# A GNN and mixture-of-experts layer on one core: VectorE's steps rearranged and shortened, and 40 result scatters kept in DRAM and replayed on the POOL queue at the end of the gather stage

## What is computed

```python
edge_index = jnp.stack([src, dst])            # 100000 edges over 6250 nodes, sorted by dst
x = x + _L0_gnn_ref(_layernorm(x, axis=-1), edge_index, L0_gnn_weight, L0_gnn_bias)
x = x + _L0_ffn_ref(_layernorm(x, axis=-1)[None], L0_ffn_gate_w, ..., L0_ffn_b2)[0]

# _L0_gnn_ref(x, ...), D = 256
    summed = jax.ops.segment_sum(x[src], dst, num_segments=n)
    deg = jax.ops.segment_sum(jnp.ones_like(src, dtype=x.dtype), dst, num_segments=n)
    agg = summed / jnp.maximum(deg, 1.0)[:, None]
    out = jnp.concatenate([x, agg], axis=-1) @ weight
    out = out / jnp.linalg.norm(out, axis=-1, keepdims=True)
    return out + bias
# _L0_ffn_ref(h, ...): 8 experts, F = 1024, a capacity for each expert
    probs = jax.nn.softmax(x @ gate_w + gate_b, axis=-1); idx = jnp.argmax(probs, axis=-1)
    pos = (jnp.cumsum(one_hot, axis=0) * one_hot).sum(-1).astype(jnp.int32) - 1
    buf = zeros.at[idx, pos_safe].set(x, mode='drop')
    hmid = jax.nn.relu(jnp.einsum('ecd,edf->ecf', buf, w1) + b1[:, None, :])
    ybuf = jnp.einsum('ecf,efd->ecd', hmid, w2) + b2[:, None, :]
    y_tok = ybuf[idx, pos_g] * (prb * kept)[:, None]
```

## Time and profile before

| | |
|---|---|
| time, median of 3 runs | 1400.24 us (1398.0 to 1404.33) |
| profiled execution | 1398.44 us, span 1396.6 us |
| TensorE busy | 1120.8 us (80%) |
| POOL busy | 907.4 us (65%) |
| VectorE busy | 868.0 us (62%) |
| ScalarE busy | 464.5 us (33%) |

### The profile page before, as it was taken

How to read it: one execution, slowest core, us unless ns; L and a number is a source line. 1 busy time by engine, 2 the same in 40 slices (tenths; PEclk the granted TensorE clock), 3 DMA queues, 4 the chain that set the end, 5 groups by cost and what they waited for, 6 DMA issues and landing times.

```text
span 1396.6 us, 29269 instructions
## 1 busy us (share of the span) xinstructions
PE 1120.8 (80%) x4989; PEld 820.2 (59%) x4990; DVE 868.0 (62%) x3856; ACT 464.5 (33%) x1360; POOL 907.4 (65%) x931
## 2 busy tenths in 40 slices
PE   1076766788889898989888898989898888887786
PEld 1054554566666666666666666666666666654454
DVE  8645454666666666666666666666666666665443
ACT  3511212233333333333333333333333333334342
POOL 3167676677777777777777777777777777731101
PEclk9999798999999999999999999999999999999999
DMA  7686878443444434343433434343434344321111
GB/s 246 199 269 206 249 226 243 148 127 116 131 123 123 130 118 133 115 132 114 128 115 112 121 110 121 110 126 110 125 110 121 114 113 120 113 75 43 47 38 35
DMA packets 113601, 183.38 MB, mean 131 GB/s; under 512 B 21419, under 2 KB 84448, under 8 KB 113584
## 3 DMA queue, kind: packets, MB, share of 16 engines
q0 software_dynamic: 43328, 109.52, 27.2%
q1 hardware_dynamic: 70256, 73.69, 17.6%
HBM read 155.29 MB, written 35.83 MB: 137 GB/s over the span
## 4 chain that ended last, share of the span: by engine, by line
DVE 29%; PE 27%; DVEq 20%; issue 18%; DMA 3%; ACT 2%; ACTq 0%; SPq 0%; POOLq 0%; POOL 0%
PE ps_q L726 14%; PE ps_h L792 7%; DVE sel L1037 6%; DVEq L1301 6%; PE ps_t L800 2%; PE ps_b L811 2%; DVE acc L1046 2%; DVEq L1108 2%; DVEq L894 2%; DMA b_b<-in_L_ffn_b 2%; DVEq L1037 1%; DVEq L1064 1%; DVE row L1150 1%; DVE idx L1033 1%; DVE bn L1156 1%
## 5 line engine op out<-in xcount | busy, mean ns | idle before, releaser
L461 POOL DMA_INDIRECT ring<-xn_d,idx x784 | 788.0, 1005 | 316.5 <-issue 171.5
L726 PE MATMUL ps_q<-ring,sel 128*128 128x257 f32 x1952 | 582.8, 405 | 151.2 <-DVE sel L1037 119.9
L726 PEld LDWEIGHTS ps_q<-ring,sel 128*128 128x128 f32 x1952 | 346.5, 195 | 291.5 <-issue 234.3
L1037 DVE SCALAR_TENSOR_TENSOR sel<-lane,block,dst_t 128x512 f32<-128x512 bf16 x245 | 184.3, 752 | 132.8 <-issue 76.6
L811 PE MATMUL ps_b<-w_sb,hid_t 128*128 x832 | 213.8, 385 | 16.1 <-ACT hid_t L626 16.1
L1046 DVE TENSOR_TENSOR acc<-acc,ps_q 128x257 f32 x245 | 103.2, 421 | 178.4 <-issue 166.9
L792 PE MATMUL ps_h<-w_sb,hid_t 128*128 x416 | 200.0, 608 | 6.2 <-ACT hid_t L594 6.2
L811 PEld LDWEIGHTS ps_b<-w_sb,hid_t 128*128 128x128 f32 x832 | 153.5, 190 | 49.0 <-issue 30.1
L621 ACT ACTIVATE hid<-ps_h 128x512 f32<-128x512 f32 x104 | 62.1, 597 | 190.4 <-PE ps_h L792 190.4
L626 ACT ACTIVATE hid_t<-ps_t,b_t 128x128 f32<-128x128 f32 x416 | 113.2, 383 | 31.5 <-PE ps_t L800 31.5
L792 PEld LDWEIGHTS ps_h<-w_sb,hid_t 128*128 128x128 f32 x416 | 75.5, 191 | 67.4 <-issue 65.2
(11 more groups left out here) (194 smaller groups left out, 1230.0 us busy)
## 6 DMA issues: line engine op xcount, KB each, us to landing
w_sb<-in_L_ffn_w SPq DMA_DIRECT2D x32, 512.0 KB, 9.7
ring<-xn_d,idx POOLq DMA_INDIRECT x784, 2.8
disp_d<-hid SPq DMA_DIRECT2D x8, 1040.0 KB, 7.9
xs<-disp_d SPq DMA_DIRECT2D x53, 130.0 KB
ys<-disp_d SPq DMA_DIRECT2D x53, 130.0 KB
b_b<-in_L_ffn_b SPq DMA_DIRECT2D x53, 128.0 KB
xb<-in_x SPq DMA_DIRECT2D x51, 128.0 KB
out<-row SPq DMA_DIRECT2D x51, 128.0 KB
```

Of the source, the lines that this page charges most:

```text
L461: pool.indirect_dma_start(ring[:, (k % 2) * TQ + j, 0:D], None, xn_d[:, :], bass.IndirectOffsetOnAxis(ap=idx[:, k * TQ + j:k * TQ + j + 1] ...
L726: mm = pe.matmul(ps[:, 0:AW], sel[:, s, j, :], ring[:, (k % 2) * TQ + j, 0:AW], start=(j == 0), stop=(j == TQ - 1), skip_group_check=True)
L1037: dve.scalar_tensor_tensor(out=sel[:, s, :, :], in0=lane[:, :].rearrange("p (j m) -> p j m", j=1).to_broadcast((P, TQ, P)), scalar=block0[ ...
```

## The change

1. **VectorE's register loads.** `dve.load(next_regs, ...)` of eight values at each trip's start goes; each `select_quad` loads the two values of the next quad right after its last selection. TensorE loads two values in each quad instead of eight in one.
2. **Index copies** (L1033, four per trip) go to ScalarE, as two copies per trip.
3. **route** has five steps in place of nine; the copy of the rows to be sent goes to ScalarE (in `exponent`). The square-root refinement of `new_row` goes: ScalarE does four small steps instead. The scaling of the bias by the gate goes to ScalarE (`out_bias`), and `result` has seven steps in place of eight.
4. **choose and finish_row move** from the earlier chains into one chain with `new_row`, behind `select_quad(t, 3)`.
5. **`down` waits** for `count_read` (VectorE has read the counts) in place of `row_ready`. TensorE's `plan` stays as it was, but for the register loads.
6. **Results of the 41 chunks of the gather stage** no longer go through POOL: SP stores each into a DRAM list (`res_d`). At the end of the gather stage POOL loads them back, seven buffers in the ring's place, and scatters 40 of them: 10 ahead of the first late dispatch, 12, 12 and 6 behind the last three dispatches and their results.
7. ScalarE's `prepare_node` moves from a trip's start to the end of the trip before.

```diff
-            def load_ys(t):
+            def keep_result(t):
+                sp.wait_ge(res_ready, chunks(t))
+                sp.dma_start(res_d[ds((t - C0) * P, P), :], ys[:, :]).then_inc(res_kept, 16)
+
+            def load_ys(t, kept=False):
...
-                if not isinstance(t, int):
-                    sp.wait_ge(res_out, 16 * chunks(t))
+                if kept:
+                    sp.wait_ge(res_kept, 16 * chunks(t))
+                elif not isinstance(t, int):
+                    sp.wait_ge(res_out, 16 * (chunks(t) - KEPT))
...
+            def load_replay(r):
+                s, use = r % NRB, r // NRB
+                if use:
+                    pool.wait_ge(replay_out[s], 16 * use)
+                pool.dma_start(rbuf[:, s, :], res_d[(r + 1) * P:(r + 2) * P, :]).then_inc(replay_in[s], 16)
+
+            def replay(r):
+                s, use = r % NRB, r // NRB
+                pool.wait_ge(replay_in[s], 16 * (use + 1))
+                pool.sem_inc(pool_turn, 1)
+                pool.indirect_dma_start(
+                    out[:, :], bass.IndirectOffsetOnAxis(ap=rbuf[:, s, C_NODE:C_NODE + 1].bitcast(I32), axis=0),
+                    rbuf[:, s, 0:D], None, bounds_check=N - 1, oob_is_err=False).then_inc(replay_out[s], 16)
+
+            def replays(part):
+                for r in range(REPLAYS[part - 1] if part else 0, REPLAYS[part]):
+                    replay(r)
+                    if 2 <= r and r - 2 + NRB < KEPT - 1:
+                        load_replay(r - 2 + NRB)
...
-            scatters(TRIPS - 1)
+            scatters(TRIPS - 1, chunk=False)
+            pool.wait_ge(ring_free, 2 * TQ + NQ * TQ)
+            pool.wait_ge(res_kept, 16 * KEPT)
+            for r in range(NRB):
+                load_replay(r)
+            replays(0)
...
+            for part, rows in ((1, P), (2, P), (3, LAST)):
+                scatters(pool.snap(t_reg), rows=rows)
+                pool.reg_add(t_reg, t_reg, 1)
+                replays(part)
...
             def exponent(t):
                 act.wait_ge(logit_ready, t + 1)
-                act.activation(g8[:, 1, :], g8[:, 0, :], ACT.Exp, bias=sm[:, 16:17],
-                               accum_out=sm[:, 17:18]).then_inc(exp_ready, 1)
+                act.activation(g8[:, 1, :], g8[:, 0, :], ACT.Exp, scale=-1.0, bias=sm[:, 16:17],
+                               accum_out=sm[:, 17:18])
+                if not isinstance(t, int):
+                    act.wait_ge(disp_out, 16 * t)
+                act.activation(sent[:, :], row[:, :], ACT.Copy).then_inc(exp_ready, 1)
...
                             pe.wait_ge(y_read, c)
                             if prev:
-                                pe.wait_ge(row_ready, t + 1)
+                                pe.wait_ge(count_read, t + 1)
...
                 select(q, k % 2, to)
+                dve.load(ends_of, qtab[0:1, ds(t * QS + k + 1, 1), :])
...
                 def s1():
                     dve.tensor_tensor(g8[:, 6, :], g8[:, 6, :], hot[:, :], ALU.mult)
-                    dve.tensor_tensor(seen[:, :], ps_b[:, D + EX:D + 2 * EX], seen[:, :], ALU.add)
+                    dve.tensor_tensor(seen[:, :], ps_b[:, D + EX:D + 2 * EX], seen[:, :], ALU.add
+                                      ).then_inc(count_read, 1)
...
                 if quads:
-                    dve.load(next_regs, qtab[0:1, ds(t * QS + QS, QS), :])
                     dve.wait_ge(cat_ready, t + 1)
                     add_last(t, 0)
                     select_quad(t, 1)
-                chains(route(t) if prev else [], choose(t, whole=prev) if chunk else [],
-                       send_copy(t) if prev else [])
-                if quads:
+                    chains(route(t))
                     add_last(t, 1)
                     select_quad(t, 2)
-                chains(result(t, node) if chunk else [],
-                       ([nothing] if chunk else []) + finish_row(t) if prev else [])
-                if quads:
+                    if chunk:
+                        chains(result(t, node))
                     add_last(t, 2)
                     select_quad(t, 3)
-                    for now, then in zip(regs, next_regs):
-                        dve.reg_mov(now, then)
-                if node:
-                    new_row(t)
-                if quads:
+                    chains(new_row(t, known), choose(t) if chunk else [], [nothing] + finish_row(t))
                     add_last(t, 3)
-                if node:
                     normalise_row(t)
-                if quads:
                     select_quad(t + 1, 0)
-                if node and next_node:
                     prepare_node(t + 1, next_known)
```

More of the change, by code:

```diff
@@ L215, in gnn_moe_layer @@
         count_ps = sem("count_ps")
+        count_read = sem("count_read")
         row_ready = sem("row_ready")
@@ L234, in gnn_moe_layer @@
         res_out = sem("res_out")
+        res_kept = sem("res_kept")
+        replay_in = [sem(f"replay_in{s}") for s in range(NRB)]
+        replay_out = [sem(f"replay_out{s}") for s in range(NRB)]
         block = ctx.enter_context(nc.Block())
@@ L524, in _ @@
             results(pool.snap(t_reg))
-            pool.wait_ge(res_out, 16 * (pool.snap(t_reg) - C0 + 1))
+            pool.wait_ge(res_out, 16 * (pool.snap(t_reg) - C0 + 1 - KEPT))
+            for s in range(NRB):
+                pool.wait_ge(replay_out[s], 16 * len(range(s, KEPT - 1, NRB)))
         @block.scalar
@@ L596, in late_trip @@
                     row_norm(t)
-                hidden(c, e)
+                hidden(c, 0)
+                if not prev:
+                    out_bias(c)
+                hidden(c, 1)
+                relus(c, e)
                 if node:
                     next_row(t)
+                    if next_node:
+                        prepare_node(t + 1, next_known)
             def chunk_rows(c):
@@ L654, in trip @@
                 if chunk:
-                    hidden(c, e)
+                    hidden(c, 0)
+                act.wait_ge(count_ps, t + 1)
+                gather_rows(t + 1, 0)
+                if chunk:
+                    hidden(c, 1)
+                    relus(c, e)
                 next_row(t)
-            with act.Fori(0, C0) as t:
+                prepare_node(t + 1, next_known)
+            prepare_node(0)
+            trip(0, chunk=False)
+            with act.Fori(1, C0) as t:
                 trip(t, chunk=False)
@@ L757, in load_expert, with load_quad @@
                     expert.append(pe.snap(code[1], min_val=0, max_val=EX - 1))
-                def load_quads():
-                    pe.load(next_regs, qtab[0:1, ds(t * QS + QS, QS), :])
-                def turn_quads():
-                    for now, then in zip(regs, next_regs):
-                        pe.reg_mov(now, then)
+                def load_quad(k):
+                    pe.load(ends_of, qtab[0:1, ds(t * QS + k, 1), :])
                 def cat_transposes():
@@ L843, in steps @@
                     return run
-                plan = [[steps((prev, gate), (chunk, load_expert)),
+                plan = [[steps((prev, gate), (chunk, load_expert), (quads, load_quad, 1)),
                          steps(),
@@ L848, in trip @@
                          steps()],
-                        [steps((node, linear, 0)),
+                        [steps((node, linear, 0), (quads, load_quad, 2)),
                          steps((node, linear, 1)),
@@ L852, in trip @@
                          steps()],
-                        [steps((prev, counts), (chunk, up, 1), (quads, load_quads)),
+                        [steps((prev, counts), (chunk, up, 1), (quads, load_quad, 3)),
                          steps((chunk, hid_transposes, 0)),
@@ L856, in trip @@
                          steps((chunk, down, (0, 1)))],
-                        [steps((chunk, down, (2, 3))),
+                        [steps((chunk, down, (2, 3)), (quads, load_quad, 4)),
                          steps((chunk, down, (4, 5))),
                          steps((chunk, down, (6, 7))),
-                         steps((node, xl_transposes), (quads, turn_quads))]]
+                         steps((node, xl_transposes))]]
                 if quads:
@@ L1169, in normalise_row @@
                 dve.drain().then_inc(stat2_ready, 1)
-            def send_copy(t):
-                def copy():
-                    if not isinstance(t, int):
-                        dve.wait_ge(disp_out, 16 * t)
-                    dve.tensor_copy(sent[:, :], row[:, :])
-                return [nothing, copy]
             def route(t):
```

216 lines of the change are left out of this document (119 added, 97 removed).

## The result

The changed kernel took 1608.77 us (median of 4 runs, 1607.31 to 1614.31), the kernel before 1399.12 us beside it (4 runs, 1397.47 to 1404.33). The ratio is 1.150, 95% interval 1.146 to 1.154. The profiled execution took 1614.31 us, 1612.5 of it span.

The account below looks back on a forecast made before the run. VectorE and TensorE were taken to set the 24.05 us trip, POOL 0.25 us behind. Span: 1396.6 + 158 (36 stalled trips) - 8 (five others) - 6 (first eight) + 24 (late stage) = 1564.6; time 1568 us, range 1485 to 1625.

Parts of the forecast that it names:

- The move of finish_row decides: Gather stage: down waits for counts now read behind quad 3's selections; two-block trips take 4.4 us more, +158 us in all.
- The count of 36 from the sorted edges: Gather stage: quad 3 holds two blocks, so down waits, in 36 of the 41 trips with a chunk.
- The stall of 4.75 us: TensorE at down, end of quad 2: idle 4.75 us until VectorE has read the counts, in two-block trips.
- The low clock, 2.3 us: TensorE's matmuls behind the stall run at low clock, 2.3 us more per trip; bounds nothing and 3.1.
- first rival (clock stays high): Gather stage: the stall is there but the 2.3 us are not, 83 us less, 1485 us; chance 12%.
- Selections, 2.1 us back: Chunk trip: VectorE's selections come earlier, saving 2.1 of the 2.27 us TensorE waits; bounds nothing and 2.4.
- free under the stall's cover: Trip's start: prepare_node ahead of the gate's copy on ScalarE costs nothing after the stall, about 1 us without it.
- the sum, 28.5: Chunk trip with two blocks in quad 3: 24.05 - 2.1 - 0.5 + 4.75 + 2.3 = 28.5 us.
- Five trips at POOL's floor of 22.5: Gather stage: the five chunk trips without the stall fall to POOL's own 22.5 us, 5 x -1.5 = -8 us.
- The first eight trips, -6: Gather stage's start, without down: earlier selections and register loads gain 6 us; between 0 and -12.
- The late stage, +24: Late stage: POOL's 40 loads and scatters delay dispatches, the last by 22 us; +24 us, bounds +10 and +38.
- The row of 2.8 us: Late stage: a 130 KB load from POOL lands in 2.8 us, so the first scatter has no wait.

Follow-up runs that it names:

- e1: Changed kernel with finish_row back behind quad 2's selections and choose back beside route, as in the kernel before; 0.995 of the kernel before, 0.990 taken again as e1r.
- e3: Changed kernel with TensorE's down matmuls placed later, behind tiles of quad 3's last visit, VectorE's order kept; 1.010 of the kernel before, 1.009 taken again.
- e2: Kernel before with one edit, finish_row moved behind quad 3's selections; 1.024 of the kernel before.
- e4: Changed kernel with 18 matmuls whose result nobody reads ahead of down's wait in each chunk trip; 1.055 of the kernel before, 1.047 taken again.
- e7: Changed kernel with e1's edits, ScalarE's gate copy ahead of prepare_node, and quad 1's pair loaded one step later; 0.978 of the kernel before.
- e8: e7 with 1, 6, 6, 6 scatters around the late dispatches and 21 in threes behind seven chunk trips' results; 0.962 of the kernel before, 0.968 taken again.

## Why the prediction was right

The time (1608.8) lies in the range, 41 us above the value, and the direction came by the mechanism that was named. Part of the closeness is luck: two terms of the chunk trip were mis-sized in opposite directions, as the account under "Selections" shows. By its steps, in the profile beside the earlier trace rows:

- **The move of finish_row decides**: shown. e1 and e3 each take the wait away from a different side; e2 makes it in the old kernel. The count of 36 from the sorted edges is the trace's 36.
- **The stall of 4.75 us**: 4.81 (923.01 to 927.82). It could be worked out from the old trace since the steps were only put behind one another.
- **The low clock, 2.3 us**: the rows behind the wait are longer by 2.7 and 1.6 us in alternate trips (0.94 for `down`, and 1.75 or 0.68 for the ten visit rows), 2.15 on average; so the first rival (clock stays high) is out. By the Trainium skill, "TensorE: Matmul & The Clock Gate", Part 1, where activity releases the high clock, the trace agrees: 0.52 and 0.64 behind the wait. Of the engine's two levels, 0.50 (1.2 GHz) and 1.00, the first window is nearly all at the lower and the second for the larger part. When the gap was filled (e4) these rows ran at the high clock, but the trip did not get shorter.
- **Selections, 2.1 us back**: their waits did go. What I missed is that 1.4 us came anew at the trip's start: the gate behind `prepare_node` (0.5 to 0.6) and the two register loads in one step (0.8). I had called `prepare_node` free under the stall's cover and 1 us without it. It was 0.5 with the cover. These numbers don't simply add. TensorE's own account closes: idle 6.2 us in place of 2.7 (+3.5) and busy 22.3 or 23.4 in place of 21.3 (+1.5 on average), together the 29.0 of a stalled trip. The forecast had +2.15 of idle time (4.75 - 2.1 - 0.5) and +2.3 of slow rows: 1.3 too little and 0.8 too much, so the sum, 28.5, was only 0.5 off. With the first two trips, 32.2 and 31.1 us, that is 23 us over the 36; another 2 come from the forecast's own rounding (36 times 28.5 - 24.05 is 160, not 158).
- **Five trips at POOL's floor of 22.5**: wrong. The step that failed is the count of POOL's own work as the trip's only bound. Four trips took 24.0 to 24.1; the last, without quads of a next trip, 21.0 (21.8 before), so 7 us of the 8 did not come. The third of the four trips' gaps, beside the two at the start, is 1.2 us ahead of quad 3's visits, for VectorE's addition (changed kernel, TensorE):

```profile
1384.24 2.44 PE L810 MATMUL ps_q<-ring,sel 128*128 128x257 f32 x10 [1.20 <-DVE acc L1121]
1387.59 0.61 PE L904 MATMUL ps_b<-gatew_sb,cat_t 128*128 128x8 f32 x4 [0.91 <-ACT cat_t L714]
1389.00 1.13 PE L810 MATMUL ps_q<-ring,sel 128*128 128x257 f32 x4 [0.79 <-issue]
```

  These three, 2.9 us, take the place of the 2.3 us of selection waits. POOL has a gap of its own there: once per trip, behind another trip without the stall, it stands 2.3 us ahead of quad 2's first gather, where 0.3 is the rule. The kernel has this gather wait for the index copy that the change gave to ScalarE (L609), behind `prepare_node` and the gate's copy; the copy ends at 1223.73 (no run tests this):

```profile
1224.86 1.25 POOL L480 DMA_INDIRECT ring<-xn_d,idx  x1 [2.26 <-issue]
```

  e7 has no stall either, and there POOL waits for TensorE, 210.8 us in 1000 (waits of e7, 300 to 1300 us), so POOL's own work is not what sets its trips:

```profile
POOL ring L480 <- PE ps_q L813: 210.8, 131, 4.8
```
- **The first eight trips, -6**: +5.8. They have no wait at `down`. TensorE's rows are busy 135.9 us in place of 129.0, at a clock of 0.83 in place of 0.86, which is as much as the whole difference; which of the changed steps lowered the clock is open.
- **The late stage, +24**: +30. The first late dispatch came 12.4 us later (12 foretold), the fourth 29 (22). Of the 7 us between, some 4 came ahead of the second dispatch (38.5 us behind the stage's start, 34 foretold), the rest in the pairs: a pair of load and scatter took 1.88 us, not 1.8, and some scatters waited for a landing. The first scatter waited 1.03 us for its load, where the forecast had no wait. The loads' median time from issue to landing (view of the DMA issues, columns as in the earlier trace rows):

```profile
ring<-res_d POOLq DMA_DIRECT2D x40, 130.0 KB, 2.5
```

  The row of 2.8 us that the forecast took was near. By the Trainium skill, "DMA: Bandwidth & Descriptors", anatomy of a SWDGE DMA, the estimate is 2.3 us, and the trace's median of 2.5 is 0.2 above it. e8 shows the scatters ahead of the dispatches as the cause of 16 to 18 us of the 30. The rest is not told apart; TensorE's rows are busy 6 us longer there, at a clock of 0.87 in place of 0.94.

Sum of the differences from the forecast: chunk trips +32 (182 against 150), late stage +6, first eight trips +12; 50 us, less the 1.7 by which the first gate came earlier: the 48 us between the span foretold (1564.6) and the one measured (1612.5).

## What to carry to other kernels

Before a step is moved down an engine's list, write out who waits for it and what that waiter has queued behind itself: if the step's new place needs anything from that queue, the wait is as long as the whole detour. Either order could be kept here, only not both. And a long stall hides others: after removing it, read the trace again at once, for the next wait (here ScalarE's copy and two register loads at a trip's start) takes part of the gain. A forecast for the time without the stall must count every engine's waits at that place, not only the work of one. Work that has slack belongs behind the late stage's critical issues in small portions, not in a block ahead of them.

## What the runs showed of the hardware

- Short gaps came with a lower clock too. In this trip of e1r TensorE has gaps of 0.8, 1.6 and 0.8 us within 5 us at the trip's start and no longer one there, and the granted clock behind them is low (windows of e1r):

```profile
710.00:715.00 5.00, 3.88 (x18) 3.26 (x19) 3.58 (x20) 2.09 (x7) 2.71 (x3) 0.78 0.39 114
715.00:720.00 5.00, 5.00 (x18) 3.77 (x19) 2.49 (x7) 1.51 (x9) 3.49 (x4) 0.88 0.34 99
```

  The Trainium skill, "TensorE: Matmul & The Clock Gate", section "A second HAM failure mode: psum-queue depth-cycling", tells of short idle pieces between groups of matmuls that bring the low clock; this trace agrees, with 0.78 and 0.88. In the kernel before, gaps of 0.76 us (ahead of 815.59) and 1.32 us (ahead of 820.10) left the clock at 1.00:

```profile
814.00:826.00 12.00, 9.78 (x48) 1.00 0.49 133
```

- The same program took 7.5% longer when it was run again (1608.8 and 1729.5 us), the kernel before 16 to 18% on all four chips of the experiments; on which chip the first measurement ran is not known. In the changed kernel all of it lies ahead of the late stage (180.2 us in place of 179.8). In these traces an engine sometimes goes on microseconds after the instruction that it waited for; the profile then calls the releaser "remote", which neither first profile does. In e1, VectorE and ScalarE both waited for `counts` (L914), which ended at 908.43, and both went on at about 913.1, while TensorE's own queue ran on:

```profile
908.26 0.17 PE L914 MATMUL ps_b<-hot,ones 128*128 128x8 bf16 x1
...
913.05 0.17 DVE L1190 TENSOR_TENSOR g<-ps_b,seen 128x8 f32<-128x8 f32 x1 [4.53 <-remote]
...
913.16 0.21 ACT L609 ACTIVATE idx<-src_t 128x8 int32 x1 [3.91 <-remote]
```

  What delays it is open; no run here touches it.
